# Latent attention in a vision tower: values formed per image, instead of probabilities meeting the latents first

## The reference, cut to what matters

```python
c_kv = h @ w_down_kv.T                      # [tokens, 128]
v = (c_kv @ w_up_v.T).reshape(b, s, H, DH)  # 16 heads of 64
attn = softmax(scores)
out = einsum('bhqk,bhkd->bhqd', attn, v)
out = out.reshape(b, s, H * DH) @ w_out.T + residual
```

## Time and profile before

| what | value |
|---|---|
| three runs | 1104.77, 1113.37, 1116.05 us; median 1113.37 |
| profiled execution | 1114.32 us, span of its instructions 1112.5 us |
| mean granted clock of TensorE | 0.888 of 2.4 GHz |
| PE, PEld busy | 909.6 us (82%), 674.0 us (61%) |
| DVE, ACT, POOL busy | 606.8, 527.1, 335.2 us |
| instructions | 26159 |

### The profile page before, as it was taken

How to read it: one execution, slowest core, us unless ns; L and a number is a source line. 1 busy time by engine, 2 the same in 40 slices (tenths; PEclk the granted TensorE clock), 3 DMA queues, 4 the chain that set the end, 5 groups by cost and what they waited for, 6 DMA issues and landing times. The chain is left out here.

```text
span 1112.5 us, 26159 instructions
## 1 busy us (share of the span) xinstructions
PE 909.6 (82%) x10336; PEld 674.0 (61%) x10336; DVE 606.8 (55%) x1306; ACT 527.1 (47%) x940; POOL 335.2 (30%) x426
## 2 busy tenths in 40 slices
PE   4889958389999789958996299999478998989564
PEld 4878735267777557647885144444267777777332
DVE  3566746656666469764664524232655573542585
ACT  2354638366656379735452155554123333442354
POOL 1203320545544100021323315442254553432101
PEclk8999958699999979879997599999799998989775
DMA  5300020200000000001001963222320000000001
GB/s 181 118 3 2 3 105 15 80 1 2 1 0 1 12 35 0 1 4 47 3 3 54 392 225 73 40 47 41 73 81 3 2 3 2 3 3 1 1 1 44
DMA packets 23973, 47.40 MB, mean 43 GB/s; under 512 B 4386, under 2 KB 15640, under 8 KB 23221
## 3 DMA queue, kind: packets, MB, share of 16 engines
q1 hardware_dynamic: 19524, 39.09, 10.1%
q0 software_dynamic: 4336, 6.74, 3.3%
HBM read 38.35 MB, written 7.47 MB: 41 GB/s over the span
## 5 line engine op out<-in xcount | busy, mean ns | idle before, releaser
L2731 PE MATMUL psum<-L2f_EW,weights_even 128*64 x176 | 83.0, 616 | 2.9 <-ACT weights_even L2430 2.1
L2732 PE MATMUL psum<-L2f_W,weights_even 128*64 128x512 f32 x176 | 83.0, 616 | 0.0
L2391 POOL DMA_INDIRECT expert_sums<-weights_even,L2f_target x20 | 36.5, 1825 | 77.8 <-DVE weights_even L2613 68.4
L2626 DVE TENSOR_TENSOR weights_even<-psum,weights_even 128x512 f32<-128x512 f32 x22 | 15.2, 692 | 77.1 <-PE psum L2732 75.1
L1057 PE MATMUL psum<-L_cT,weights_odd 128*128 128x222 f32 (+1 forms) x192 | 45.2, 366 | 12.7 <-DVE L_by_sin L944 11.0
L2438 ACT ACTIVATE L2f_W<-L2f_EW 128x1024 f32 x44 | 46.3, 1053 | 15.4 <-DMA L2f_EW<-experts 8.2
L2247 PE MATMUL psum<-weights_even,L1f_H 128*111 128x256 f32 x176 | 47.3, 427 | 7.4 <-DVE L1f_H L2178 7.4
L2731 PEld LDWEIGHTS psum<-L2f_EW,weights_even 128*64 128x64 f32 x176 | 22.9, 140 | 46.6 <-issue 46.6
L419 ACT ACTIVATE L_PT<-psum 101x296 f32<-101x296 f32 x64 | 27.0, 421 | 48.2 <-PE psum L615 48.1
L876 ACT ACTIVATE L_U<-psum 128x592 f32<-128x592 f32 x32 | 21.2, 663 | 60.0 <-PE psum L1108 60.0
L2247 PEld LDWEIGHTS psum<-weights_even,L1f_H 128*111 128x111 f32 x176 | 35.1, 202 | 18.7 <-DVE L1f_H L2178 8.7
(11 more groups left out here) (459 smaller groups left out, 2627.2 us busy)
## 6 DMA issues: line engine op xcount, KB each, us to landing
L2f_EW<-experts SPq DMA_DIRECT2D x24, 512.0 KB, 7.4
weights_even<-L_w SPq DMA_DIRECT2D x4, 1024.0 KB
patch_ring<-patches SPq DMA_DIRECT2D x11, 333.0 KB
expert_sums<-L_blank SPq DMA_DIRECT2D x1, 1184.0 KB
out<-X SPq DMA_DIRECT2D x10, 111.0 KB
weights_odd<-L_wo SPq DMA_DIRECT2D x1, 1024.0 KB
expert_rows<-X SPq DMA_DIRECT2D x1, 960.0 KB
expert_sums<-X SPq DMA_DIRECT2D x1, 960.0 KB
```

The source lines that it names most:

```text
L2731: nc.tensor.matmul(core.bank(bank)[PAIR[0], :], xsT[:, j % 2, c, PAIR[0]], own, start=c == 0, stop=c == KD - 1)
L2732: mm = nc.tensor.matmul(core.bank(bank)[PAIR[1], :], xsT[:, j % 2, c, PAIR[1]], cols(W1[:, part], KD, NF)[:, c], start=c == 0, stop=c == K ...
```

## The change

`naturals`, `gather`, `nat_out`, `u_out` and the tiles `c_nat` and `U` go. A new `v_project` forms the values of a pair, token by feature, 16 heads of 64 at once: 4 matmuls, each with the latents of one image (128 x 37 of `cT`) as stationary matrix and 512 columns of `wuv` as moving one, into two banks (`VB`). It stands right behind the scores of the same pair. ACT `v_out` copies both banks to `V` (two buffers), between the two halves' `p_T` and `c_out`. `values` now multiplies `V` with the transposed probabilities, per image and head: 16 matmuls a half instead of 8, with 37 rows, 64 stationary and 37 moving columns; in twos, one on the upper left quarter of the array and one on the lower right. One memset of the gap rows of `VB` is added on DVE ahead of the loop. Waits follow the new buffers.

```diff
+                def v_out(s):
+                    act.wait_ge(v_ps, s + 1)
+                    after(act, o_ps, 2 * (s - 1))
+                    nc.scalar.activation(V[:PR, s % 2], core.psum[:PR, VB:VB + 2, :], ACT.Copy).then_inc(v_done, 1)
...
                     if s >= 1:
                         p_T(s - 1, 1)
+                    if s < NP:
+                        v_out(s)
                     if k == 2 and u + 2 < NU:
                         c_out(u + 2)
                     if s >= 1:
-                        u_out(s - 1, 0)
-                        u_out(s - 1, 1)
                         o_T(s - 1, 0)
-                    if s + 3 < NP:
-                        nat_out(s + 3)
-                    if s >= 1:
                         o_T(s - 1, 1)
...
+                nc.vector.memset(core.psum[32:64, VB:VB + 2, :], 0.0).then_inc(gaps_set, 1)
...
                 def latents(u):
                     pe.wait_ge(xT_done, u + 1)
-                    after(pe, c_done, min(u, 1))
-                    after(pe, nat_done, 3 * u - 1 if u > 1 else 0)
+                    after(pe, c_done, u)
+                    after(pe, z_done, projected(3 * (u - 2) + 1))
...
-                def naturals(s):
...
+                def v_project(s):
+                    u = unit_of(s)
+                    pe.wait_ge(c_done, u + 1)
+                    pe.wait_ge(gaps_set, 2)
+                    after(pe, v_done, s)
                     for b in range(2):
-                        for kd in range(KD):
-                            for e in range(2):
-                                mm = nc.tensor.matmul(core.bank(M2)[64 * e:64 * e + T, b * 128:(b + 1) * 128], xT[:, u % 2, kd, own(2 * s + b)], wdkv[:, kd, :],
-                                                      start=kd == 0, stop=kd == KD - 1)
-                    mm.then_inc(nat_ps, 1)
+                        for e in range(2):
+                            mm = nc.tensor.matmul(cols(core.bank(VB + b)[64 * e:64 * e + T, :], 8, 64), cT[:, u % 2, 1, own(2 * s + b)], wuv_of[:, e],
+                                                  start=True, stop=True)
+                    mm.then_inc(v_ps, 1)
...
-                def gather(s, half):
...
+                def values(s, half):
                     pe.wait_ge(pt_done, 2 * s + half + 1)
-                    pe.wait_ge(nat_done, s + 1)
...
-                def values(s, half):
-                    pe.wait_ge(u_done, 2 * s + half + 1)
+                    pe.wait_ge(v_done, s + 1)
                     after(pe, oT_done, 2 * s + half)
                     for i in range(4):
-                        for e in range(2):
-                            head = 2 * (4 * half + i) + e
-                            mm = nc.tensor.matmul(core.bank(M3)[64 * e:64 * e + 64, 2 * i * T:2 * (i + 1) * T], wuv[:, 64 * head:64 * (head + 1)],
-                                                  U[:, half, e, 2 * i * T:2 * (i + 1) * T], start=True, stop=True)
+                        cq = 4 * half + i
+                        for b in range(2):
+                            for e in range(2):
+                                rows = slice(64 * e, 64 * e + T)
+                                mm = nc.tensor.matmul(core.bank(M3)[64 * e:64 * e + 64, (2 * i + b) * T:(2 * i + b + 1) * T],
+                                                      V[rows, s % 2, b, 64 * cq:64 * (cq + 1)], PT[rows, s % 2, cq, b * T:(b + 1) * T], start=True, stop=True)
                     mm.then_inc(o_ps, 1)
...
                 def o_project(t, s):
                     u, k = unit_of(s), s % 3
                     pe.wait_ge(oT_done, 2 * pairs_for(t))
-                    pe.wait_ge(nat_done, min(s + 3, NP))
-                    if k == 2 and u + 2 < NU:
-                        pe.wait_ge(c_done, u + 3)
+                    pe.wait_ge(c_done, min(u + 3 if k == 2 else u + 2, NU))
...
                     if s < NP:
                         score(s, 0)
                         score(s, 1)
+                        v_project(s)
...
                     if s >= 1:
-                        gather(s - 1, 0)
+                        values(s - 1, 0)
                     if s in TILE_AT and (k != 1 or s == NP):
                         o_project(TILE_AT[s], s)
                     if late:
                         up(*late[0])
-                    if s >= 1:
-                        gather(s - 1, 1)
                     if s == NP:
                         weights_T(3)
                     if s >= 1:
-                        values(s - 1, 0)
+                        values(s - 1, 1)
                     if s == NP:
                         weights_T(4)
-                    if s + 3 < NP:
-                        naturals(s + 3)
-                    if s >= 1:
-                        values(s - 1, 1)
                     if len(late) > 1:
                         up(*late[1])
```

More of the change, by code:

```diff
@@ L726, in latent_attention @@
     NC2 = 2 * R
-    S0, PTB, UB, M1, M2, M3 = 0, 2, 3, 5, 6, 7
+    S0, PTB, VB, M1, M2, M3 = 0, 2, 3, 5, 6, 7
     NQK, RING = 8, 12
@@ L738, in latent_attention @@
         qT, kT = sb("qT", [128, 2, 4, 2, NC2]), sb("kT", [128, 2, 4, 2, NC2])
-        c_nat = sb("c_nat", [128, 6, 2, 128])
-        U = sb("U", [128, 2, 2, 8 * T])
+        V = sb("V", [128, 2, 2, 512])
         P = sb("P", [128, 2, 16, 64])
@@ L747, in latent_attention @@
         pstat, pmv, prs = sb("pstat", [128, 2, 6]), sb("pmv", [128, 2, 2]), sb("prs", [128, 2])
[L748 to L751, removed]
+        (pvar, x_staged, xT_ps, xT_done, c_ps, c_done, qk_ps, turned, rotated, v_ps, v_done, half_ps, s_ps, shifted, exp_done, sum_ready, p_ready,
+         pt_ps, pt_done, o_ps, oT_done, y_ps, z_done, var_ready, norm_done, zeroed, gaps_set) = st.sems(
+            "pvar x_staged xT_ps xT_done c_ps c_done qk_ps turned rotated v_ps v_done half_ps s_ps shifted exp_done sum_ready p_ready "
+            "pt_ps pt_done o_ps oT_done y_ps z_done var_ready norm_done zeroed gaps_set")
         p_scales, p_scaled, p_quantised, pT_ps, pT_done = st.sems("p_scales p_scaled p_quantised pT_ps pT_done")
@@ L754, in latent_attention @@
         wuq, wuk, wuv = w["L3_wuq"], w["L3_wuk"], w["L3_wuv"]
+        wuv_of = wuv.rearrange("p (c e d) -> p e c d", c=8, e=2)
         wo = cols(w["L3_wo"], 8, D)
@@ L851, in x_T @@
                     after(act, c_ps, u - 1)
-                    after(act, nat_ps, pairs_of(u - 1))
                     n = len(UNITS[u][1])
@@ L865, in c_out @@
                     act.wait_ge(c_ps, u + 1)
+                    after(act, v_ps, pairs_of(u - 1))
                     nc.scalar.activation(cT[:, u % 2, :, 0:width(u)], cols(core.bank(M2)[:, 0:2 * NC2], 2, NC2)[:, :, 0:width(u)], ACT.Copy).then_inc(c_done, 1)
[L868 to L876, removed]
+                def v_out(s):
+                    act.wait_ge(v_ps, s + 1)
+                    after(act, o_ps, 2 * (s - 1))
+                    nc.scalar.activation(V[:PR, s % 2], core.psum[:PR, VB:VB + 2, :], ACT.Copy).then_inc(v_done, 1)
                 def exps(s):
@@ L883, in p_T @@
                     act.wait_ge(pt_ps, 2 * s + half + 1)
-                    after(act, u_ps, 2 * (s - 1))
+                    after(act, o_ps, 2 * (s - 1))
                     nc.scalar.activation(PT[:PR, s % 2, 4 * half:4 * half + 4].rearrange("p n (b q) -> p n b q", b=2),
@@ L897, in _ @@
                 c_out(1)
-                for p in range(3):
-                    nat_out(p)
                 for s in range(NP + 1):
@@ L1059, in up @@
                     mm.then_inc(qk_ps, 1)
-                def naturals(s):
[L1062 to L1067, removed]
-                    for b in range(2):
-                        for kd in range(KD):
-                            for e in range(2):
-                                mm = nc.tensor.matmul(core.bank(M2)[64 * e:64 * e + T, b * 128:(b + 1) * 128], xT[:, u % 2, kd, own(2 * s + b)], wdkv[:, kd, :],
-                                                      start=kd == 0, stop=kd == KD - 1)
-                    mm.then_inc(nat_ps, 1)
+                def v_project(s):
[3 more added lines that the diff above has]
+                    after(pe, v_done, s)
+                    for b in range(2):
+                        for e in range(2):
+                            mm = nc.tensor.matmul(cols(core.bank(VB + b)[64 * e:64 * e + T, :], 8, 64), cT[:, u % 2, 1, own(2 * s + b)], wuv_of[:, e],
+                                                  start=True, stop=True)
+                    mm.then_inc(v_ps, 1)
                 def score(s, rows2):
@@ L1099, in p_T @@
                     mm.then_inc(pt_ps, 1)
-                def gather(s, half):
+                def values(s, half):
                     pe.wait_ge(pt_done, 2 * s + half + 1)
-                    pe.wait_ge(nat_done, s + 1)
-                    after(pe, u_done, 2 * s + half)
-                    for b in range(2):
-                        for e in range(2):
```

(11 more changed lines are left out.)

## The result

The changed kernel takes 1114.81 us in the median of 18 runs (1110.44 to 1126.43), the kernel before 1109.72 in 18 runs beside them. The ratio is 1.0056 [1.0031, 1.0081]: slower by about 6.2 us, and within 1%, as forecast. The forecast sum was +1.0 us; some 5 us are not in it. The profiled execution took 1110.44 us.

The account below looks back on a forecast made before the run. PE was taken as the bound, its time and waits deciding. Terms +0.3 - 0.2 - 0.55 + 0.95 + 1.6 - 1.1 summed to +1.0 us, a median of 1114.4 us; the range ran from 1103 to 1127 us.

Parts of the forecast that it names:

- Prices: On PE, `v_project` was put at 1.74 us and a half of `values` at 1.00 us.
- the rival at 1154 us: In `v_project` the column halves don't overlap, +2.5 us on each of 16 turns; chance 0.03.
- The rival in which the small matmuls run like the scores: New `values` matmuls at 14 ns each, 0.45 us a half; 1103.4 us in all; chance 0.16.
- The row of another stage with 28 ns: A matmul of nearest shape, 64 rows, 60 stationary and 30 moving columns, used to price `values` at 30 ns an instruction.
- Order: `v_project` ahead of the first `up` shifts the calls in a turn: k = 0 +0.1 us, k = 1 and k = 2 0.0.
- three regular units: Regular turns at k = 0, 1 and 2, three times over: 3 x 0.1 = +0.3 us.
- Tail: Last three pairs, where `naturals` was already over: +1.6 us; last turn, with cheaper `values` and a covered wait: -1.1 us.
- they wait for POOL to 824.08, -0.55: At the head, the first scores start earlier without the three `naturals`, waiting only for POOL: -0.55 us.
- about +0.95: First turn, with no `values` to fill the waits between calls of `up`: about +0.95 us.
- The rival of the clock: Clock falls more often where a `turn` wait and two `values` meet; 1131.4 us, or 1122.9 if half; chance 0.20.
- as many stretches at 1.2 GHz: Sign in the profile after: the stage has as many stretches at 1.2 GHz as before.
- five stretches of before: Stretches at 1.2 GHz behind the stage's head, each behind small matmuls or waits; put at 8.5 us in all.

Follow-up runs that it names:

- e7: The changed kernel with 32 instead of 64 stationary columns in each new `values` matmul, as many instructions; median 1104.56 us, 0.9945 of the kernel before.
- e3: The changed kernel with `v_project` moved from behind the scores into PE's waits between calls of `up`; median 1114.05 us, 1.0013 of the kernel before.
- e1: The changed kernel with a filler, 64 matmuls never read, on PE ahead of the first scores; median 1109.55 us, 0.9986 of the kernel before.
- e2: The kernel before with its three `naturals` ahead of the loop cut from 16 instructions to 2 each; median 1109.36 us, 0.9962 of the kernel before.
- e5: The changed kernel with one image's half of `v_project` kept behind the scores, the other in PE's waits; median 1107.66 us, 0.9946 of the kernel before.
- e4: The changed kernel with `v_project` moved into PE's waits and the filler ahead of the first scores; median 1112.51 us, 0.9981 of the kernel before.
- e6: The changed kernel with `v_project` split by image and the filler ahead of the first scores; median 1105.98 us, 0.9934 of the kernel before.
- e8: The kernel before with each of its three `naturals` ahead of the loop computed twice; median 1116.24 us, 1.0062 of the kernel before.

## Why the prediction was right, and where it was short

- **Prices.** `v_project` 1.84 us (1.74 in the sum), `values` 1.05 (1.00), `v_out` 1021 ns (1.02 us). That the column halves overlap holds; the rival at 1154 us is out. The Trainium skill (TensorEngine Tiling (Array Packing), Instruction Overhead) has a fixed overhead of about 60 cycles, an estimated 25 ns at 2.4 GHz, so that a matmul with one column costs as much as one with 60. As a floor the trace does not bear it out: the scores take 14 ns an instruction and the `values` of e7 21. A half of `values` is 1.05 us with 64 stationary columns and 0.67 with 32, at the same count of instructions and of moving columns.
- **The rival in which the small matmuls run like the scores** (14 ns) is out: they take 33 ns. The row of another stage with 28 ns was the right neighbour.
- **Order.** The second `up` came at 4.59 us (4.46). The turns moved by +0.29, +0.13 and +0.08 us (0.1, 0, 0), so three regular units cost +1.5 where the sum has +0.3. ACT lost 13.3 us in the stage (66.19 against 79.47; 11 foreseen), and nothing came of it; no turn waited for `v_out`. At full speed the change costs 0.4 to 1.5 us, across chips, against a sum of +1.0. The place behind the scores leaves about 8 us at full speed to be had (e3), most of it in waits that the kernel before has as well.
- **Tail.** Last turn -1.0 us (-1.1). The turns of the last three pairs cost +1.1 (+1.6): two of them 27.90 us against 27.29, and the third with the last turn 24.63 against 25.12, of which the last is -1.0. But the two turns were granted 0.84 of full speed, before 0.87, which makes 27.90 x 0.16 - 27.29 x 0.13 = 0.9 us of the difference: at one clock the tail's turns cost nearly nothing, and the +1.6 is not borne out.
- **The term that was short** is the head, "they wait for POOL to 824.08, -0.55", with "about +0.95" for the first turn. The wait ended nearly where it was put: from the last calls of `up` to the scores are 6.94 us, 7.33 before, -0.39 (the scores begin 0.15 us behind POOL's end). The turns were sized well too: in e1, where the clock holds, the first two take 9.22 and 10.64 us against 7.98 and 10.75, so +1.24 and -0.11. But the sum took 3.77 us of idle PE for free, and the first scores ran at 1.2 GHz after it: in all five profiled kernels with an empty or nearly empty head (after, e2, e3, e5, e7) 64 instructions of the first scores take 1.26 or 1.27 us (2.49 for 128), in all five with work there (before, e1, e4, e6, e8) 0.85 to 0.87. In the profile of after the first two turns cost 8.3 us more, where the sum has +0.95 and -0.2. Over the runs the size is not settled (e2, e8).
- **The rival of the clock** was half right. It looked for falls where `turn` and two `values` meet. That "as many stretches at 1.2 GHz" would be seen did not hold, but in the profile the place was the head (behind the first two turns the granted clock is 0.96, before 0.95), and over the runs the size 2.9 to 3.9 us, not 8 to 17. Its five stretches of before are 10.2 us and not 8.5: the last is 8.70 us long at 0.61. The stage's granted clock moved by 0.02, inside the 0.03 allowed.
- **Luck.** The median of 1114.81 lies 0.4 us from the 1114.4 on record. That is chance: three runs of before had a median of 1113.37, 18 runs have 1109.72. The forecast to judge is the difference, +1.0, and +6.2 was measured.

**Open.** How much of the 5.7 to 7.7 us at 1.2 GHz belongs to the head. The filler takes 18.6 ± 4.1 us in the changed kernel, 10.6 ± 4.1 in the split one, 6.1 ± 5.6 in the moved one, and emptying the old head added none (-1.8 ± 3.6). That filling gains in the changed kernel is settled; its size is not. The profile of e1 gains on that of after at the head and not behind it: from there on the granted clock is 0.96 in both. How often the clock falls at the head in the runs of each kernel is not known, with one profile a kernel.

## What to carry to other kernels

When work is removed, ask what it covered: here three small calls at the head were the only thing that PE did during a wait. Without them the new order lost its clock there, and putting such work back gained 7.8 us (e1), more than the steady turns cost; in the old order their removal cost nothing over the runs (e2). Split a kernel's runs into time at 1.2 GHz and the rest before comparing variants, since a better order (e3, 8.0 us at full speed) can give part of its gain back to the clock (3.3 ± 2.2 us there). In this kernel the work with full-height stationary matrices did best divided: part behind the small matmuls, part in the waits (e5, e6).

## What the runs showed of the hardware

- Small matmuls on two opposite quarters of the array cost more with more stationary columns, 33 ns an instruction with 64 and 21 ns with 32 (37 rows, 37 moving columns), while scores with 32 rows, 37 stationary and 37 moving columns take 14 ns.
- The runs of a kernel differ mostly in their time at 1.2 GHz: from run to run it has a standard deviation of 8 to 13 us, the full-speed time one of 2 to 3 us. A microsecond more at 1.2 GHz goes with 0.40 us more of time.
- After 3.8 us of idle PE the first scores ran at 1.2 GHz in four profiles of four (after, e3, e5, e7); with work there they ran at 2.4 GHz in five of five, but in e8 the clock still fell within the first two turns.
